# One batch alone ahead of the first scores: the other batches' first norms go into the unit loop of a decoder kernel

## The chip, the core and the metric

The kernel runs on one core of a Trainium2 chip. The metric is the device time of one launch in microseconds (us). A core has five engines that run their own instruction streams and wait for each other at semaphores: TensorE (PE: matrix products and transposes into PSUM), VectorE (DVE), ScalarE (ACT: activations, also plain copies), GpSimd (POOL) and SyncE (SP), which here only issues DMA transfers.

## The reference, cut to what matters

Six sublayers follow each other, each with a residual and a layer norm without weights in front. x is 4 batches of 512 rows of 128 numbers. Only the start of the first sublayer matters here:

```python
x = x + _L0_attn_ref(_layernorm(x, axis=-1), W_in, b_in, W_out, b_out)

P = X @ W_in + b_in                        # 16 heads, each with Q, K, V, G of 64
d2 = q2[..., :, None] + k2[..., None, :] - 2.0 * qk
W = jnp.power(EPS + jnp.sqrt(jnp.maximum(d2, 0.0)), -2)
W = W / (EPS + jnp.sum(W, axis=-1, keepdims=True))
A = jnp.einsum('hbts,hbse->hbte', W, V)
H = G * A                                  # then heads side by side, @ W_out + b_out
```

q2 and k2 are the squared norms of the rows of Q and K. After it come a cross attention, a mixture of experts with its own attention, a windowed attention, a second cross attention and a quantized feed-forward layer; the change doesn't touch them.

## The kernel before, in words

The first sublayer runs in 32 units: a unit is one batch and one pair of heads, batch by batch, so units 0 to 7 read batch 0 alone, units 8 to 15 batch 1, and so on. The normalized and transposed rows of all batches lie in `XT` (128 numbers on the partitions, 512 rows per batch).

For a unit TensorE makes K, Q, V and G by projections from `XT[:, b]` (`project_pair`, `project_values_and_gates`), the squared norms q2 and k2 (`query_norms`, `key_norms`), the scores in eight PSUM banks (`scores`: first a product with the split q2 in bf16, then Q against K), the weighted values and the row sums of the weights of the unit before, and from unit 2 on a piece of the output projection. VectorE evacuates K and Q and forms their squares (`evacuate_pair`, four operations), evacuates V and G, and adds k2 to the scores and clips them (`guard`, eight operations of 128x512, called guards below). ScalarE takes root, logarithm and exponential of the 128x4096 distances of a unit in six passes, changes its function table twice in each unit, and takes the reciprocal of the row sums in the same way. GpSimd splits q2 into three bf16 pieces (`split_norms`, four operations), adds up the weights of a unit for the row sums (`sum_weights`, three operations) and scales the gates.

The projections of unit u + 2 stand behind the scores of unit u in the loop; those of unit 1 stand in unit 0, also behind the scores. The squares of Q go through one buffer, and so does the copy of q2 (`QX`).

The order on each engine is written out by hand: each engine has a function that issues its instructions in program order, and nothing is reordered. `psum_jobs` lists all uses of PSUM banks in TensorE's order; `place_jobs` gives them banks in turn and works out which semaphores a use must wait for until its bank has been read.

Ahead of the loop every engine works on all four batches of the first layer norm (numbered `(0, b)`): VectorE forms statistics (`stats`) and normalizes (`normalize`), ScalarE makes the reciprocal deviation from the variance (`rstd`, one logarithm, one exponential), TensorE transposes (`ln_turn`), ScalarE copies to `XT` (`xt_out`). GpSimd adds the output bias to the rows of `X` once they have been normalized (line 2741). SyncE issues the transfers on one queue in program order: batch 0, the constants, batches 1 to 3, the biases, the weights of head pair 0, then the value bias `BV` and the weights of the seven other pairs.

`after_batch(u, n)` names the batch whose last unit lies n + 1 units back; by it later norms already stand inside the loop.

## Time and profile before

| what | us |
|---|---|
| median of 3 runs (1272.89 to 1273.5) | 1272.97 |
| the profiled execution | 1272.73 |
| its span in the trace | 1270.8 |
| busy: TensorE, VectorE, ScalarE, GpSimd | 1128.9, 901.9, 879.7, 627.9 |
| first transposes, first projection, first scores (start) | 9.45, 16.11, 27.59 |
| scores of units 1, 2 (start) | 48.60, 63.91 |

The profiled execution has 1.9 us outside its span. The page cuts the span into 40 slices of 32 us; the busy share of a slice stands as a digit in tenths. In the first slice TensorE has a 4, in the second an 8, and from there a 9 until the unit loop ends near 560 us:

```profile
PE   4899999999999999987888898799997999985765
DVE  5766667766767677657888978546746786878885
ACT  2799999999989998992666767755564676733311
POOL 2577777777767777595455545013330300054232
```

### The profile page before, as it was taken

How to read it: one execution, taken by the hardware profiler on the slowest of the kernel's cores; microseconds unless marked ns; L12 is line 12 of the kernel's file. 1: busy time of each engine (PE TensorE's matmuls, PEld its weight loads, DVE VectorE, ACT ScalarE, POOL GpSimd, SP SyncE). 2: the span in 40 equal slices, each digit the busy share in tenths (PEclk: the TensorE clock that was granted, in tenths of full speed). 3: DMA queues.
4: the chain of work that ended last, by engine and by line, in shares of the span. 5: the costliest groups of instructions: out<-in, count | busy, mean ns of one | idle time of the engine just before them, and what ended most of it. 6: DMA issues, size and time to landing. Idle time of an engine off the chain costs nothing.

```text
span 1270.8 us, 17038 instructions
## 1 busy us (share of the span) xinstructions
PE 1128.9 (89%) x6055; PEld 589.1 (46%) x6055; DVE 901.9 (71%) x1756; ACT 879.7 (69%) x1150; POOL 627.9 (49%) x463
## 2 busy tenths in 40 slices
PE   4899999999999999987888898799997999985765
PEld 2444444444444444432333332277775676653444
DVE  5766667766767677657888978546746786878885
ACT  2799999999989998992666767755564676733311
POOL 2577777777767777595455545013330300054232
PEclk9999999999999999996889989999998999997877
DMA  7200000000000000020000000000001000000000
GB/s 178 66 1 2 1 1 1 1 1 1 1 1 1 1 1 1 1 68 1 18 1 1 1 1 1 2 1 1 1 1 63 1 1 1 1 1 0 1 9 25
DMA packets 25631, 14.47 MB, mean 11 GB/s; under 512 B 14558, under 2 KB 24396, under 8 KB 25420
## 3 DMA queue, kind: packets, MB, share of 16 engines
q1 hardware_dynamic: 25548, 13.39, 3.7%
q8 instruction: 49, 0.80, 0.2%
q14 instruction: 34, 0.28, 0.1%
HBM read 12.34 MB, written 1.05 MB: 11 GB/s over the span
## 4 chain that ended last, share of the span: by engine, by line
PE 31%; POOL 31%; issue 20%; DVE 16%; ACT 1%; DMA 0%; POOLq 0%; SPq 0%; ACTq 0%; DVEq 0%
DVE ARENA L1159 6%; POOL ARENA L2711 6%; POOL ARENA L2709 6%; POOL ARENA L2705 6%; PE PS L1030 5%; POOL WQ L2722 3%; POOL ARENA L2735 3%; PE PS L900 3%; PE PS L1414 2%; PE PS L1004 2%; PE PS L832 2%; PE PS L1438 2%; PE PS L848 2%; PE PS L1405 2%; POOL WQ L2724 2%
## 5 line engine op out<-in xcount | busy, mean ns | idle before, releaser
L2565 DVE TENSOR_SCALAR ARENA<-PS,ARENA 128x512 f32<-128x512 f32 x256 | 174.5, 744 | 66.7 <-PE PS L2199 66.3
L1159 DVE TENSOR_REDUCE ARENA<-PS 128x1 f32<-128x512 f32 x256 | 160.9, 683 | 28.2 <-PE PS L848 27.7
L1075 ACT ACTIVATE ARENA<-PS 128x1024 f32<-128x1024 f32 x128 | 128.9, 1026 | 61.9 <-PE PS L886 61.6
L2378 ACT ACTIVATE ARENA<-ARENA 128x2048 f32<-128x2048 f32 x64 | 122.2, 1912 | 60.6 <-DVE ARENA L2565 60.1
L2199 PE MATMUL PS<-ARENA 64*128 64x512 f32 x512 | 129.0, 623 | 0.0
L2385 ACT ACTIVATE ARENA<-ARENA,consts_sb 128x2048 f32<-128x2048 f32 x64 | 124.6, 1994 | 0.4
L2209 PE MATMUL PS<-ARENA 128*64 128x512 f32 x512 | 118.7, 606 | 1.3 <-issue 1.3
L2391 ACT ACTIVATE ARENA<-ARENA 128x2048 f32<-128x2048 f32 x64 | 118.4, 1898 | 0.0
L2718 POOL TENSOR_SCALAR WQ<-ARENA,consts_sb 128x512 bf16<-128x512 f32 x32 | 22.3, 696 | 159.1 <-DVE ARENA L2541 159.1
L1340 POOL TENSOR_TENSOR ARENA<-ARENA 128x512 f32<-128x512 f32 x32 | 40.7, 1271 | 121.4 <-DVE ARENA L1298 120.9
L848 PE MATMUL PS<-ARENA 32*128 32x512 bf16 x256 | 74.0, 415 | 24.9 <-DVE ARENA L1159 19.8
L2541 DVE TENSOR_SCALAR ARENA<-PS 128x512 f32<-128x512 f32 x32 | 22.1, 692 | 95.3 <-PE PS L2175 95.3
L900 PE MATMUL PS<-ARENA 128*32 128x512 f32 x512 | 73.2, 645 | 8.9 <-issue 7.9
L2711 POOL TENSOR_TENSOR ARENA<-ARENA 128x1024 f32<-128x1024 f32 x32 | 76.0, 2375 | 2.5
L2709 POOL TENSOR_TENSOR ARENA<-ARENA 128x1024 f32<-128x1024 f32 x32 | 75.8, 2370 | 0.0
L2705 POOL TENSOR_TENSOR ARENA<-ARENA 128x1024 f32<-128x1024 f32 x32 | 75.7, 2365 | 0.0
L2209 PEld LDWEIGHTS PS<-ARENA 128*64 128x64 f32 x512 | 34.7, 138 | 81.1 <-issue 81.1
L1312 POOL TENSOR_SCALAR ARENA<-ARENA,consts_sb 128x512 bf16<-128x512 f32 x32 | 21.8, 695 | 100.3 <-ACT ARENA L1057 100.3
L1030 PEld LDWEIGHTS PS<-W,ARENA 128*128 128x128 f32 x512 | 59.5, 191 | 21.2 <-issue 19.0
L1106 ACT ACTIVATE ARENA<-PS,ARENA 128x512 f32<-128x512 f32 x64 | 40.4, 684 | 37.4 <-PE PS L1004 37.4
L1030 PE MATMUL PS<-W,ARENA 128*128 128x128 f32 x512 | 65.3, 281 | 0.8 <-ACT ARENA L1106 0.7
L848 PEld LDWEIGHTS PS<-ARENA 32*128 32x128 bf16 x256 | 17.5, 92 | 104.3 <-DVE ARENA L1159 64.0
(301 smaller groups left out, 2606.3 us busy)
## 6 DMA issues: line engine op xcount, KB each, us to landing
ARENA<-in_window_bias_dram SPq DMA_DIRECT2D x1, 1536.0 KB, 6.3
WKVG<-in_L_attn_W_in_dram SPq DMA_DIRECT2D x3, 448.0 KB, 5.6
X<-in_x_dram SPq DMA_DIRECT2D x4, 256.0 KB, 5.4
W<-in_L_ffn_w_dram SPq DMA_DIRECT2D x1, 1024.0 KB
out_dram<-X SPq DMA_DIRECT2D x4, 256.0 KB, 2.3
BV<-in_L_attn_b_in_dram SPq DMA_DIRECT2D x1, 512.0 KB, 6.7
Wout<-in_L_attn_W_out_dram SPq DMA_DIRECT2D x1, 512.0 KB, 4.7
WQ<-in_L_attn_wq_dram SPq DMA_DIRECT2D x1, 512.0 KB, 3.3
```

Source lines behind the costliest of these rows:

```text
L1030: mm = pe.matmul(o[:, t * P:(t + 1) * P], H1[:, i % 2, c, t * P:(t + 1) * P], W2[:, e, c, :], start=c == 0, stop=c == 1)
L1075: act.activation(PT[m % PT_SLOTS], bank(("cP", m)), ACT.Exp, scale=0.5).then_inc(sem("c_exp"), 1)
L1159: dve.tensor_reduce(NMX[:, w % 2, t, h:h + 1], bank(("cS", n, j)), AX.X, ALU.max, negate=True).then_inc(sem("c_max"), 1)
L2199: done(pe.matmul(banks[c], SK[r, u % 2, kt * P:(kt + 1) * P], MQ[r, u % 2, :], start=False, stop=True), ("S", u, c))
L2209: mm = pe.matmul(o[hd * 64:hd * 64 + 64, :], VA[:, u % 3, kt, hd * 64:hd * 64 + 64], D[:, u % 2, kt, hd, :], start=kt == 0, stop=kt == QT - 1)
L2378: act.activation(chunk(u, half), chunk(u, half), ACT.Sqrt).then_inc(sem("rooted"), 1)
L2385: act.activation(chunk(u, half), chunk(u, half), ACT.Ln, bias=const("eps_w")).then_inc(sem("logged"), 1)
L2391: act.activation(chunk(u, half), chunk(u, half), ACT.Exp, scale=-2.0).then_inc(sem("w_ready"), 1)
L2565: dve.tensor_scalar(D[:, u % 2, kt, hd, :], bank(("S", u, c)), K2[:, u % 2, kt, hd:hd + 1], 1e-30, ALU.add, ALU.max).then_inc(sem("guarded ...
L2705: pool.tensor_tensor(WSUM[:, u % 2], D[:, u % 2, 0], D[:, u % 2, 1], ALU.add).then_inc(sem("w_paired"), 1)
L2709: pool.tensor_tensor(WPAIR, D[:, u % 2, 2], D[:, u % 2, 3], ALU.add).then_inc(sem("w_paired"), 1)
L2711: pool.tensor_tensor(WSUM[:, u % 2], WSUM[:, u % 2], WPAIR, ALU.add).then_inc(sem("w_summed"), 1)
```

## The change

Only batch 0 goes through its first norm ahead of the loop. A new function `first_norm(u, units_after)` gives the batch whose first norm has a step in unit u: statistics in units 0, 1, 2 (batches 1, 2, 3), the deviation in units 1, 2, 3, normalization in units 2, 3, 4, transposes and copy in units 3, 4, 5; GpSimd's bias addition too in units 3, 4, 5. The projections of unit 1 and VectorE's evacuation of them stand ahead of the scores of unit 0 instead of behind them; its norms q2 and k2 stay behind. GpSimd splits the norms of unit 1 ahead of the bias addition and the clearing of three buffers (the `memset` lines), and those of unit 2 behind them. SyncE takes the weights of head pair 1 as a transfer group of its own (`win_next_in`), and issues batches 1 to 3 behind it, ahead of the weights of pairs 2 to 7. ScalarE loads its function table ahead of the wait for the constants. Batch 3 is normalized into the room of batch 0 in `Y`, since its own room holds the squares of Q.

```diff
+def first_norm(u, units_after):
+
+    b = u - units_after + 1
+    return b if 1 <= b < B else None
...
-            for heads, name in ((slice(0, 2), "win_first_in"), (slice(2, H0), "win_in")):
-                if name == "win_in":
+            for heads, name in ((slice(0, 2), "win_first_in"), (slice(2, 4), "win_next_in"), (slice(4, H0), "win_in")):
+                if name == "win_next_in":
...
+                if name == "win_next_in":
+                    for b in range(1, B):
+                        stream_in(b)
...
             def project_pair(u):
                 b, p = divmod(u, PAIRS)
+                if p == 0:
+                    pe.wait_ge(sem("xt_ready"), norm_no(0, b))
...
             pe.wait_ge(sem("consts_in"), 16)
-            for b in range(B):
-                ln_turn(0, b)
+            ln_turn(0, 0)
...
             key_norms(0)
+            pe.wait_ge(sem("win_next_in"), 16 * 4)
+            project_pair(1)
             pe.wait_ge(sem("pieces_set"), 1)
             for u in range(UNITS):
                 scores(u, 0)
                 scores(u, 1)
                 if u == 0:
-                    pe.wait_ge(sem("win_in"), 16 * 4)
-                    project_pair(1)
                     query_norms(1)
                     key_norms(1)
+                    pe.wait_ge(sem("win_in"), 16 * 4)
...
+                if first_norm(u, 3) is not None:
+                    ln_turn(0, first_norm(u, 3))
...
+                if first_norm(u, 1) is not None:
+                    rstd(0, first_norm(u, 1))
+                if first_norm(u, 3) is not None:
+                    xt_out(0, first_norm(u, 3))
...
+            act.preload_act_table_set("natural_log_exp_and_others")
             act.wait_ge(sem("consts_in"), 16)
-            act.preload_act_table_set("natural_log_exp_and_others")
-            for b in range(B):
-                rstd(0, b)
-            for b in range(B):
-                xt_out(0, b)
+            rstd(0, 0)
+            xt_out(0, 0)
...
-            layernorm(0)
+            stats(0, 0)
+            normalize(0, 0)
...
-            full(dve, ("ln", 0, B - 1))
...
             key_norms(0)
+            evacuate_pair(1)
...
                 if u == 0:
-                    evacuate_pair(1)
...
+                if first_norm(u, 0) is not None:
+                    stats(0, first_norm(u, 0))
+                if first_norm(u, 2) is not None:
+                    normalize(0, first_norm(u, 2))
...
             split_norms(0)
+            split_norms(1)
...
             pool.wait_ge(sem("bcast_in"), 32)
-            for b in range(B):
-                pool.wait_ge(sem("ln_y"), b + 1)
...
-            pool.wait_ge(sem("x_biased"), B)
+            add_bias(0)
             for t in (WX, VC0, TMX):
                 pool.memset(t, 0.0).then_inc(sem("c_init"), 1)
-            for u in range(1, 3):
-                split_norms(u)
+            split_norms(2)
             for u in range(UNITS):
                 sum_weights(u)
+                if first_norm(u, 3) is not None:
+                    add_bias(first_norm(u, 3))
```

GpSimd, from the end of the split of unit 0 to the start of that of unit 2, or as far as twelve rows reach; L2741 and L2760 are the bias additions, L2745 and L2766 the clearing. Before:

```order
L2728 TENSOR_TENSOR ARENA<-WQ 128x512
L2741 TENSOR_TENSOR X<-X,Bout 128x512 x4
L2745 MEMSET ARENA 128x1024
L2745 MEMSET ARENA 128x2048
L2745 MEMSET ARENA 128x1024
L2718 TENSOR_SCALAR WQ<-ARENA,consts_sb 128x512
L2722 TENSOR_TENSOR WQ<-ARENA,WQ 128x512
L2724 TENSOR_SCALAR WQ<-WQ,consts_sb 128x512
L2728 TENSOR_TENSOR ARENA<-WQ 128x512
L2718 TENSOR_SCALAR WQ<-ARENA,consts_sb 128x512
```

And on the same engine in the changed kernel:

```order
L2746 TENSOR_TENSOR ARENA<-WQ 128x512
L2736 TENSOR_SCALAR WQ<-ARENA,consts_sb 128x512
L2740 TENSOR_TENSOR WQ<-ARENA,WQ 128x512
L2742 TENSOR_SCALAR WQ<-WQ,consts_sb 128x512
L2746 TENSOR_TENSOR ARENA<-WQ 128x512
L2760 TENSOR_TENSOR X<-X,Bout 128x512
L2766 MEMSET ARENA 128x1024
L2766 MEMSET ARENA 128x2048
L2766 MEMSET ARENA 128x1024
L2736 TENSOR_SCALAR WQ<-ARENA,consts_sb 128x512
```

The split of unit 1 has moved ahead of the bias and the clearing, and three of the four bias additions are gone from here.

TensorE, from the key norms of unit 0 on (the x4 on consts_sb,ARENA); the rows on PIECES and on ARENA are the scores, XT with WKVG or WQ the projections of K and Q. Before:

```order
L2181 MATMUL PS<-consts_sb,ARENA 128x128 x4
L2195 MATMUL PS<-ARENA,PIECES 128x512 x4
L2199 MATMUL PS<-ARENA 128x512 x4
L2195 MATMUL PS<-ARENA,PIECES 128x512 x4
L2199 MATMUL PS<-ARENA 128x512 x4
L2156 MATMUL PS<-XT,WKVG 128x512
L2159 MATMUL PS<-XT,WQ 128x512
L2175 MATMUL PS<-Y,consts_sb 128x512
L2181 MATMUL PS<-consts_sb,ARENA 128x128 x4
```

On the same engine after the change:

```order
L2198 MATMUL PS<-consts_sb,ARENA 128x128 x4
L2173 MATMUL PS<-XT,WKVG 128x512
L2176 MATMUL PS<-XT,WQ 128x512
L2212 MATMUL PS<-ARENA,PIECES 128x512 x4
L2216 MATMUL PS<-ARENA 128x512 x4
L2212 MATMUL PS<-ARENA,PIECES 128x512 x4
L2216 MATMUL PS<-ARENA 128x512 x4
L2192 MATMUL PS<-Y,consts_sb 128x512
L2198 MATMUL PS<-consts_sb,ARENA 128x128 x4
```

The two projections of unit 1 have moved ahead of the scores of unit 0, and the norms of unit 1 follow the scores directly.

VectorE at the end of unit 2 in the changed kernel, from the copy of q2 of unit 4 to the guards of unit 3 (before, the copy of k2 and the guards are neighbours there):

```order
L2555 TENSOR_SCALAR ARENA<-PS 128x512
L2567 COPY ARENA<-PS 128x8
L2514 BN_STATS STAT<-X 128x6 x4
L2517 BN_AGGR MV<-STAT 128x2 x4
L2524 TENSOR_SCALAR Y<-X,MV,RSTD 128x128 x4
L2579 TENSOR_SCALAR ARENA<-PS,ARENA 128x512 x8
```

The statistics of batch 3 and the normalization of batch 1 stand between the norms and the guards.

## Rows read from the trace of the kernel before

**Rows 1.** The page's groups: line, engine, operation, count, busy us, mean ns.

```profile
L2385 ACT ACTIVATE ARENA<-ARENA,consts_sb 128x2048 f32<-128x2048 f32 x64 | 124.6, 1994 | 0.4
...
L2541 DVE TENSOR_SCALAR ARENA<-PS 128x512 f32<-128x512 f32 x32 | 22.1, 692 | 95.3 <-PE PS L2175 95.3
```

**Rows 2.** Timeline of VectorE, start: start us, us, line, operation, count, [idle before].

```profile
3.73 0.87 DVE L2493 BATCH_NORM_STATS2 STAT<-X 128x6 f32<-128x128 f32 x4 [3.73 <-DMA X<-in_x_dram]
4.64 0.38 DVE L2496 BATCH_NORM_AGGREGATE MV<-STAT 128x2 f32<-128x6 f32 x4
...
8.22 1.09 DVE L2503 TENSOR_SCALAR Y<-X,MV,RSTD 128x128 f32<-128x128 f32 x4
```

**Rows 3.** Timeline of ScalarE, start.

```profile
4.99 1.28 ACT L2441 ACT_TABLE_LOAD   x1 [4.99 <-DMA consts_sb<-in_consts_dram]
6.29 0.30 ACT L2364 ACTIVATE RSTD<-MV,consts_sb 128x4 f32<-128x4 f32 x1
...
15.92 0.59 ACT L2371 COPY XT<-PS 128x512 f32<-128x512 f32 x1 [0.44 <-PE PS L2143]
```

**Rows 4.** Timeline of TensorE, start.

```profile
9.45 1.08 PE L2143 MATMUL PS<-consts_sb,Y 128*128 128x128 f32 x4 [9.45 <-DVE Y L2503]
...
16.11 2.07 PE L2156 MATMUL PS<-XT,WKVG 128*128 128x512 f32 x2
...
27.59 0.74 PE L2195 MATMUL PS<-ARENA,PIECES 32*128 32x512 bf16 x4 [4.00 <-issue]
```

**Rows 5.** DMA issues until 45 us: count, KB each, median us to landing.

```profile
BV<-in_L_attn_b_in_dram SPq DMA_DIRECT2D x1, 512.0 KB, 6.7
...
WKVG<-in_L_attn_W_in_dram SPq DMA_DIRECT2D x3, 64.0 KB, 2.5
```

**Rows 6.** Timeline of SyncE's issues, start.

```profile
5.86 1.49 SPq L2069 DMA_DIRECT2D WKVG<-in_L_attn_W_in_dram  x3
...
9.61 7.26 SPq L2069 DMA_DIRECT2D WKVG<-in_L_attn_W_in_dram  x3
```

**Rows 7.** Timeline of GpSimd, 23 to 60 us.

```profile
23.53 0.69 POOL L2718 TENSOR_SCALAR WQ<-ARENA,consts_sb 128x512 bf16<-128x512 f32 x1 [21.67 <-DVE ARENA L2541]
...
27.45 4.93 POOL L2741 TENSOR_TENSOR X<-X,Bout 128x512 f32<-128x512 f32 x4
32.45 3.59 POOL L2745 MEMSET ARENA<- 128x1024 f32 x3
...
52.53 2.36 POOL L2705 TENSOR_TENSOR ARENA<-ARENA 128x1024 f32<-128x1024 f32 x1
```

**Rows 8.** Timeline of TensorE, units 1 and 2.

```profile
48.60 0.39 PE L2195 MATMUL PS<-ARENA,PIECES 32*128 32x512 bf16 x4
...
57.52 3.65 PE L2209 MATMUL PS<-ARENA 128*64 128x512 f32 x16
61.01 1.03 PE L2217 MATMUL PS<-ARENA,consts_sb 128*64 128x512 f32 x4
...
63.91 0.40 PE L2195 MATMUL PS<-ARENA,PIECES 32*128 32x512 bf16 x4
```

**Rows 9.** Timeline of VectorE, behind the guards of unit 1.

```profile
55.74 0.74 DVE L2518 TENSOR_SCALAR ARENA<-PS,BKP 128x512 f32<-128x512 f32 x1
```

**Rows 10.** Windows: length, busy us per engine, clock; last two: units 11, 12.

```profile
36.50:39.10 2.60, 0.01 (x1) 0.01 (x1) 2.54 (x4) 2.58 (x2) 0.00 (x0) 1.00 0.98 267
39.10:42.60 3.50, 3.50 (x11) 2.47 (x12) 0.69 (x1) 3.49 (x3) 0.70 (x1) 0.53 0.01 1
211.65:227.89 16.24, 15.97 (x78) 7.29 (x78) 11.42 (x19) 15.51 (x11) 11.98 (x9) 1.00 0.00 1
227.89:244.52 16.63, 16.36 (x82) 7.68 (x83) 12.29 (x20) 15.48 (x12) 12.19 (x9) 1.00 0.00 0
```

**Rows 11.** Timeline of VectorE around the guards of units 12 and 13.

```profile
227.19 2.20 DVE L2503 TENSOR_SCALAR Y<-X,MV,RSTD 128x128 f32<-128x128 f32 x4
...
246.10 0.75 DVE L2565 TENSOR_SCALAR ARENA<-PS,ARENA 128x512 f32<-128x512 f32 x1 [2.21 <-PE PS L2199]
```

More of the change, by code:

```diff
@@ L662, in decoder_kernel, with normal_rows @@
         QSQ = Y[:, B - 1].rearrange("p t d -> p (t d)")
+        def normal_rows(k, b):
+            return Y[:, 0 if (k, b) == (0, B - 1) else b]
         assert at <= 31412
@@ L2147, in ln_turn @@
                 pe.wait_ge(sem("ln_y"), norm_no(k, b))
-                transposes(("ln", k, b), Y[:, b])
+                transposes(("ln", k, b), normal_rows(k, b))
             def wpair(p, kind):
@@ L2737, in _, with add_bias @@
             split_norms(0)
-            pool.wait_ge(sem("bcast_in"), 32)
-            for b in range(B):
-                pool.wait_ge(sem("ln_y"), b + 1)
+            split_norms(1)
+            def add_bias(b):
+                pool.wait_ge(sem("ln_y"), norm_no(0, b))
                 pool.tensor_tensor(X[:, b], X[:, b], Bout[:].unsqueeze(1).to_broadcast([P, QT, P]),
                                    ALU.add).then_inc(sem("x_biased"), 1)
-            pool.wait_ge(sem("x_biased"), B)
+            pool.wait_ge(sem("bcast_in"), 32)
+            add_bias(0)
             for t in (WX, VC0, TMX):
                 pool.memset(t, 0.0).then_inc(sem("c_init"), 1)
-            for u in range(1, 3):
-                split_norms(u)
+            split_norms(2)
             for u in range(UNITS):
                 sum_weights(u)
+                if first_norm(u, 3) is not None:
+                    add_bias(first_norm(u, 3))
                 if u + 3 < UNITS:
```

21 lines of the change are left out of this document (8 added, 13 removed).

## The prediction

> **What bounds the kernel now.** I read the page's slices first, then the timelines of each engine over the first 80 us (where the change moves most), then windows that cut the unit loop at the starts of the scores. In the loop over the 32 units TensorE is the bound: between the scores of units 11 and 12 it works 15.97 of 16.24 us [rows 10]. So anything that reaches TensorE earlier is kept to the end, and anything added to TensorE in the loop is paid.
>
> The start isn't bound by TensorE. VectorE gets batch 0 at 3.73 us and has its statistics at 5.02 [rows 2]; ScalarE loads its table only after the constants have landed, and takes the logarithm at 6.29 [rows 3]; batch 0 is normalized at 8.22, because VectorE was on batch 1 in between [rows 2]. TensorE then turns four batches, and the first projection starts at 16.11, though it reads batch 0 alone [rows 4]. From there to the first scores (27.59) it is a chain: project, evacuate, norms, and the split on GpSimd, which starts at 23.53 [rows 4, 7]. After the scores of unit 0 the next long wait is again GpSimd: it adds the bias to four batches (4.93), clears (3.59), and splits unit 1 and unit 2 before it comes to the weights of unit 0 at 52.53. TensorE takes the row sums of unit 0 at 61.01, when GpSimd has them, and the scores of unit 2 start at 63.91 [rows 7, 8]. From there TensorE is the bound. So I work out when the scores of unit 2 start in the changed kernel, and then what units 2 to 5 cost more.
>
> **Part 1, to the first scores.** Statistics of batch 0 end at 5.02, as before. The table is now loaded ahead of the wait for the constants, so the logarithm can start when both are there, near 5.1: the table load was seen to wait until 4.99 for the constants [rows 3]. Logarithm 0.30, an exponential on the same four numbers, hand-offs: 5.7. Normalize 1.09: 6.8. Four transposes 1.08: 8.0. Copy 0.59: 8.6, and with the hand-off the first projection can start at 8.75 instead of 16.11 [rows 2 to 4].
>
> Does something else come last there? On the sync queue the three other batches are gone from ahead of the weights (three issues of half a microsecond each), so the 64 KB slices of the first pair, issued until 7.35 before, are issued until 5.8, and with the 2.5 us to landing they are there at 8.3 [rows 5, 6]. That is just ahead of 8.75. BV is needed near 14.5; issued at 5.8 to 6.3 with its 6.7 [rows 5] it lands at 13. The weights of the second pair follow behind it and are needed at 16.5 to 17.5.
>
> From the first projection to the scores it was 27.59 - 16.11 = 11.48. The chain is the same, but TensorE is at its low pace for longer, since it now comes from idle: 2.07 us for the K projection is already the low pace [rows 4] (the clock column shows no record so early; the duration tells it), and before, the pace came up in the middle of the Q projection. Now V and G can be slow too, some 0.9 each, of which VectorE's evacuation of Q covers about 0.6. So 11.75 if the pace comes up early, 12.75 if late; I take 12.25, the middle. First scores at 8.75 + 12.25 = 21.0 (20.5 to 21.5).
>
> The second unit's projections and their evacuation (four VectorE operations of up to 0.74 [rows 9]) go under GpSimd's split of 3.92 us [rows 7], where TensorE and VectorE were idle: nothing.
>
> **Part 2, from the scores of unit 0 (call it s) to those of unit 2.** The guards end 7.14 after a warm start (48.60 to 55.74) [rows 8, 9], the norms' copy takes 0.69 [rows 1], so GpSimd starts the split of unit 1 at s + 7.9. From there it never waits: split 3.96, one bias 1.24 (4.93 / 4), clears 3.6, split 4.0, three sums of 2.36 (7.15 with gaps) [rows 7]. The sum is 20.0: row sums at s + 27.9. The split of unit 2 finds its input (TensorE has made it by s + 12), and the first sum its weights: behind the guards ScalarE has one more root, a table of 1.28, two logarithms and two exponentials, none over 1.99 [rows 1, 3], so all are done by s + 18.4, and the sums begin at s + 20.8. TensorE has the scores of unit 1 at about s + 12.8 (12.41 from scores to row sums in unit 1, less 3.5 of weighted values, plus two pairs of norms, 1.9 each) and is at the row sums 12.41 later, at s + 25.3 [rows 8]: it waits 2.6 us. From the row sums to the next scores 63.91 - 61.01 = 2.9 [rows 8]. Scores of unit 2 at s + 30.9 = 51.9, against 63.91: 12.0 earlier. What was late before (four biases ahead of the split, the projections of unit 1 behind the scores) is gone; what is late next is GpSimd's own work.
>
> **Part 3, what the loop pays.** (a) Three groups of transposes more on TensorE, in units 3, 4, 5. Unit 12 has just that: 16.63 against 16.24, so 0.39 each, 1.2 in all [rows 10]. (b) On VectorE the statistics (0.87 + 0.38 [rows 2]) come behind the norms of units 0, 1, 2, and the normalization behind those of 2, 3, 4. The room there is the 2.21 us that VectorE waits for the scores [rows 11] (about 1.3 in units 0 and 1, where no output piece stands behind the norms). Statistics alone fit. A normalization in this place took 2.20 us, not the 1.09 of the start [rows 2, 11]: GpSimd splits at that time. It just fits alone (units 3 and 4; in unit 4 a small copy comes on top, 0.2), but in unit 2 both come: 1.2 + 2.2 - 2.2 = 1.2 late, between 0.1 (if it took 1.09) and 1.2; I take 1.2, the nearer row. TensorE's second half of the scores needs the banks that the guards free, so I let it pass in full. (c) ScalarE gets at most 1.1 more in a unit (a pair of small activations, a copy of 0.59), and is busy for 15.51 of 16.24, with 0.39 more to come; the bias additions (1.24) go into GpSimd's wait, 11.98 of 16.24 busy [rows 10]: nothing. Sum: 1.2 + 1.2 + 0.2 = 2.6.
>
> Here the Trainium skill bears: SBUF — State Buffer, section "SBUF: two separate sides", says that VectorE and GpSimd share one pair of ports as an exclusive lock, and that the loser is blocked for the whole instruction. The two durations of the same operation above agree with it. By that rule alone, each of the four pieces could wait for a whole GpSimd operation of 1.2 us, and unit 2 would lose up to some 4 us instead of 1.2; the measured 2.20 decides here.
>
> **Part 4, the pace.** TensorE now has two idle gaps: 2.0 us before the first scores (it has done unit 1's projections by about 19) and 2.6 before the row sums of unit 0. After the gap of 2.60 at 36.50 the granted clock fell, and 3.50 us went at about half of it (0.53) [rows 10], which costs some 1.7. I take that for the gap of 2.6, not for that of 2.0. Both ends: 0 and 3.4. The Trainium skill (TensorE: Matmul & The Clock Gate, section "Why this matters for your kernels") warns only of idle gaps longer than both of these; by it the cost would be 0 (rival A), while the row shows a fall after 2.60.
>
> **Sum.** -12.0 + 2.6 + 1.7 = -7.7. The profiled execution took 1272.73 us (0.24 under the median); 1265.0, against the median 1265.2. The rest of the program has the same instructions in the same order, shifted.
>
> **The rivals.**
> A, the pace holds in both gaps: 1.7 less, 1263.6. For it: both gaps are short, and in their stretch TensorE is busier than before. Chance 0.2.
> B, it falls in both, or in one of them while the weights land a little late: another 1.7, 1266.9. For it: the fall after 2.60. Chance 0.2.
> C, the loop swallows more: each of three batches costs what the crowded unit 2 costs and the transposes, as where VectorE holds up the scores: 3 x (1.2 + 0.39) + 2 from a normalization that waits longer beside the sums, about 6.8 instead of 2.6, so 1269.4. For it: the doubled 2.20. Against it: unit 12 costs only 0.39 with the same normalization in front of it. 0.1.
> D, slower: the weights of the pairs 2 to 7 stand behind all of the second pair's and the three batches on the sync queue, and TensorE has the projection of unit 2 right behind the norms of unit 1, at s + 7.2 = 28.2; the whole TensorE queue stands behind that wait. The issue of the 448 KB slices stalls, 7.26 us for three until 16.9 [rows 6], and with the 6.7 us of BV to landing the last is there near 23.5; the same bytes are ahead of it now. It decides only if they land after 28.2, and the gain is gone when they land 7.7 later than that, at 36; at 40 the kernel is at 1277. 0.03.
> The forecast has 0.4. The other 0.07 lies between C and no change, mostly a late landing of some part of the first weights.
>
> **How the numbers follow.** About 0.2% (2.5 us) is what a measurement of this kernel can tell from no change. The forecast, A, B and C all are faster by more: 0.90, and a part of the rest: 0.92. Within: 0.05. Slower: 0.03. The range reaches below A by the half microsecond of the first scores and a cheap unit 2: 1262.2; above to B and half way into C: 1268.8.
>
> **What would show it.** The first projection near 8.8; the first scores near 21 with VectorE's second unit done before them; GpSimd without a gap from the split of unit 1 to the sums of unit 0; TensorE waiting 2 to 3 us for them, the scores of unit 2 near 52; a wait for VectorE at the scores of unit 3 and a period 0.4 longer in units 3 to 5; from unit 6 on each start about 7.7 us earlier. Wrong would be: the first projection waiting for weights after 9.5, a wait at unit 2's projection for a DMA, or a shift that keeps shrinking after unit 5.

## The result, and the profile after

| what | before | changed kernel |
|---|---|---|
| median of 5 runs each, us | 1272.89 (1271.22 to 1273.5) | 1265.47 (1265.02 to 1266.25) |
| ratio, 95% interval | | 0.9946 (0.9933 to 0.996) |
| the profiled execution / its span, us | 1272.73 / 1270.8 | 1266.25 / 1264.4 |

The changed kernel is 7.4 us faster; 7.7 were forecast. Where the time came from is read from the starts of the scores, unit by unit, which cut the loop in both traces at the same instruction:

| start of the scores of unit | before, us | after, us | difference |
|---|---|---|---|
| 0 | 27.59 | 20.81 | -6.78 |
| 1 | 48.60 | 33.92 | -14.68 |
| 2 | 63.91 | 52.92 | -10.99 |
| 3 | 80.16 | 69.37 | -10.79 |
| 4 | 96.39 | 86.60 | -9.79 |
| 5 | 113.31 | 104.10 | -9.21 |
| 6 to 20 | 129.54 ... 361.50 | 122.37 ... 354.34 | -7.17 |
| 21 | 380.26 | 373.95 | -6.31 |
| 29 | 517.49 | 511.90 | -5.59 |
| end of the span | 1270.8 | 1264.4 | -6.4 |

11 us are won by unit 2, 3.8 are given back by unit 6. By unit 29 another 1.6 net are gone: units 20 and 28 take 0.86 and 0.99, and unit 26 gives 0.27 back. The change touches none of the three. (Unit 26 took 16.92 in the three traced kernels with all four norms ahead of the loop and 16.65 in the nine others; why wasn't followed up.)

The start, on VectorE and ScalarE in the changed kernel's timelines (start, us, engine, line, operation, count, and in brackets the idle time before and who ended it), which answers to [rows 2, 3]:

```profile
3.82 0.87 DVE L2514 BATCH_NORM_STATS2 STAT<-X 128x6 f32<-128x128 f32 x4 [3.82 <-DMA X<-in_x_dram]
4.72 0.38 DVE L2517 BATCH_NORM_AGGREGATE MV<-STAT 128x2 f32<-128x6 f32 x4
5.77 1.12 DVE L2524 TENSOR_SCALAR Y<-X,MV,RSTD 128x128 f32<-128x128 f32 x4 [0.67 <-ACT RSTD L2385]
```

```profile
0.73 1.28 ACT L2463 ACT_TABLE_LOAD   x1 [0.73 <-PEq L2791]
5.20 0.30 ACT L2383 ACTIVATE RSTD<-MV,consts_sb 128x4 f32<-128x4 f32 x1 [3.19 <-DVE MV L2517]
```

The normalization of batch 0 starts at 5.77 instead of 8.22. TensorE's timeline, which answers to [rows 4] and, from 42.84 on, to [rows 8]:

```profile
7.04 1.08 PE L2158 MATMUL PS<-consts_sb,Y 128*128 128x128 f32 x4 [7.04 <-DVE Y L2524]
...
8.89 2.05 PE L2173 MATMUL PS<-XT,WKVG 128*128 128x512 f32 x2 [0.47 <-ACT XT L2390]
...
20.81 0.40 PE L2212 MATMUL PS<-ARENA,PIECES 32*128 32x512 bf16 x4 [2.28 <-issue]
...
42.84 3.65 PE L2226 MATMUL PS<-ARENA 128*64 128x512 f32 x16
48.59 1.08 PE L2234 MATMUL PS<-ARENA,consts_sb 128*64 128x512 f32 x4 [2.10 <-POOL ARENA L2729]
49.60 1.68 PE L2192 MATMUL PS<-Y,consts_sb 128*128 128x512 f32 x2
51.07 1.91 PE L2198 MATMUL PS<-consts_sb,ARENA 128*128 128x128 f32 x8
```

The first projection waits for ScalarE's copy, not for weights. The row sums of unit 0 wait 2.10 us for GpSimd, and behind that wait the norms take 1.68 and 1.91 us, which take 1.12 and 1.05 in the second profile below: the granted clock of the stretch is 0.67 (first window below), so TensorE spent most of it at the lower of its two clock levels (1.2 and 2.4 GHz). GpSimd's timeline, which answers to [rows 7]:

```profile
28.73 0.69 POOL L2736 TENSOR_SCALAR WQ<-ARENA,consts_sb 128x512 bf16<-128x512 f32 x1 [8.02 <-DVE ARENA L2555]
...
32.67 1.28 POOL L2760 TENSOR_TENSOR X<-X,Bout 128x512 f32<-128x512 f32 x1
33.89 3.59 POOL L2766 MEMSET ARENA<- 128x1024 f32 x3
...
46.18 2.35 POOL L2729 TENSOR_TENSOR ARENA<-ARENA 128x1024 f32<-128x1024 f32 x1
```

From 28.73 to 48.5 it has no gap, but 8.02 us of idle time stand just ahead. The windows (length, then busy time of each engine, granted clock, DMA share, GB/s) are the row sums and norms behind TensorE's wait; unit 2; unit 12, which answers to the last of [rows 10]; and unit 20:

```profile
48.59:52.92 4.33, 4.33 (x16) 2.45 (x17) 0.69 (x1) 3.58 (x6) 0.73 (x2) 0.67 0.01 0
52.92:69.37 16.45, 16.18 (x77) 7.29 (x77) 12.74 (x30) 14.22 (x13) 12.04 (x9) 0.98 0.01 2
220.72:237.35 16.63, 16.36 (x82) 7.68 (x82) 12.31 (x20) 15.49 (x12) 12.11 (x9) 1.00 0.00 0
354.34:373.95 19.61, 17.84 (x81) 7.90 (x80) 14.24 (x29) 14.37 (x14) 12.05 (x9) 0.91 0.00 0
```

Unit 12 is what it was. What the loop gives back shows on VectorE, at the end of unit 2 and of unit 4; the normalizations there answer to [rows 11]:

```profile
69.86 1.79 DVE L2524 TENSOR_SCALAR Y<-X,MV,RSTD 128x128 f32<-128x128 f32 x4
71.57 2.71 DVE L2579 TENSOR_SCALAR ARENA<-PS,ARENA 128x512 f32<-128x512 f32 x4
...
103.40 2.19 DVE L2524 TENSOR_SCALAR Y<-X,MV,RSTD 128x128 f32<-128x128 f32 x4
105.51 0.18 DVE L2670 COPY BN<-PS 128x38 f32<-128x38 f32 x1
```

And on TensorE right behind (the scores of unit 5):

```profile
105.75 0.39 PE L2212 MATMUL PS<-ARENA,PIECES 32*128 32x512 bf16 x3 [1.27 <-DVE BN L2670]
```

The scores of unit 5 take their second bank from the transposed bias columns. VectorE's small copy (BN, 0.18 us) empties it, and that copy stands behind the normalization of 2.19 us.

### The profile page after: what moved, and what is told of

The parts are those of the page before. It is cut to its first block, busy times and chain, and to the rows that moved or that the text cites. A ratio compares the mean times of both kernels' runs of the same rounds, so it can differ in the third digit from the quotient of the medians.

```text
span 1264.4 us, 17047 instructions
## 1 busy us (share of the span) xinstructions
PE 1128.7 (89%) x6055; PEld 588.6 (47%) x6055; DVE 904.6 (72%) x1756; ACT 879.9 (70%) x1150; POOL 628.3 (50%) x463
## 3 DMA queue, kind: packets, MB, share of 16 engines
HBM read 12.34 MB, written 1.05 MB: 11 GB/s over the span
## 4 chain that ended last, share of the span: by engine, by line
PE 32%; POOL 31%; issue 20%; DVE 15%; ACT 1%; POOLq 0%; DMA 0%; ACTq 0%; DVEq 0%
DVE ARENA L1170 6%; POOL ARENA L2729 6%; POOL ARENA L2727 6%; POOL ARENA L2723 6%; PE PS L1041 5%; POOL WQ L2740 3%; POOL ARENA L2753 3%; PE PS L911 3%; PE PS L1425 2%; PE PS L1015 2%; PE PS L843 2%; PE PS L1449 2%; PE PS L1416 2%; PE PS L859 2%; POOL WQ L2742 2%
## 5 line engine op out<-in xcount | busy, mean ns | idle before, releaser
L2216 PEld LDWEIGHTS PS<-ARENA 64*128 64x128 f32 x512 | 44.9, 189 | 46.0 <-issue 46.0
L859 PEld LDWEIGHTS PS<-ARENA 32*128 32x128 bf16 x256 | 17.6, 92 | 104.2 <-DVE ARENA L1170 64.0
```

Of the source, the lines that this page charges most:

```text
L2216: done(pe.matmul(banks[c], SK[r, u % 2, kt * P:(kt + 1) * P], MQ[r, u % 2, :], start=False, stop=True), ("S", u, c))
```

## The experiments

All were timed in 5 rounds beside the kernel before, which gave 4 to 12 executions of each; ratios are to the kernel before, with 95% intervals. The changed kernel stands at 0.9946 (0.9933 to 0.996) in its own series and at 0.9929 (0.9915 to 0.9942) in the last one. The intervals of the variants with the clears moved, the copy ahead, the normalization ahead, both edits, and the other batches loaded first overlap one or both of the changed kernel's. Their totals don't settle a difference from it, so what they show is read from the units of one traced execution each. "Unit n" is the time from the scores of unit n to those of unit n+1.

**GpSimd's clears in its idle time.**

```diff
             split_norms(0)
-            split_norms(1)
...
             add_bias(0)
             for t in (WX, VC0, TMX):
                 pool.memset(t, 0.0).then_inc(sem("c_init"), 1)
+            split_norms(1)
             split_norms(2)
```

> The changed kernel, but GpSimd adds the bias to batch 0 and clears its three tiles (1.28 + 3.59 us) straight behind the split of unit 0, and then splits units 1 and 2. Theory: from 28.73 to the row sums at 48.59 GpSimd works without a gap and sets their start, while it idles 8.02 us before that; with 4.9 us of work moved into the idle stretch the row sums come up to the 2.1 us earlier that TensorE waits, the clock doesn't fall behind them (1.4 us in the row sums and norms of that stretch), and the split of unit 1 may start up to 0.3 later. Scores of unit 2 near 49.6 instead of 52.9; about 3.3 us less than the changed kernel, near 1262. Rival (the whole gain is the 7.2 us by which the first projection starts earlier, and what lies between first scores and unit 6 is noise of the same size): no change, 1265.5.

Measured: 1262.01 (1255.72 to 1268.16, the widest spread of all), ratio 0.9917 (0.9892 to 0.9941). The scores of unit 2 start at 49.56, 3.36 earlier, as expected: GpSimd's work between the guards and the row sums was what the changed kernel waited for. The end didn't follow: unit 3 took 19.80 instead of 17.23, and from unit 4 on the profiled execution is only 0.6 earlier. VectorE, GpSimd and TensorE there:

```profile
66.69 2.71 DVE L2524 TENSOR_SCALAR Y<-X,MV,RSTD 128x128 f32<-128x128 f32 x4
```

```profile
66.09 1.16 POOL L2740 TENSOR_TENSOR WQ<-ARENA,WQ 128x512 f32<-128x512 f32 x1
...
68.16 1.16 POOL L2746 TENSOR_TENSOR ARENA<-WQ 128x512 bf16<-128x512 f32 x1
```

```profile
70.12 0.39 PE L2212 MATMUL PS<-ARENA,PIECES 32*128 32x512 bf16 x1 [1.28 <-DVE ARENA L2579]
...
71.09 3.45 PE L2216 MATMUL PS<-ARENA 64*128 64x512 f32 x8
```

The normalization of unit 2 took 2.71 beside GpSimd's split (1.79 in the changed kernel), the guards came later by that, TensorE waited 1.28, and its scores went at 3.45 instead of 1.99. So the gain at unit 2 was right, and the total right by its median, but in the execution that the trace shows the loop swallowed 2.8 of the 3.4 us, 2.6 of them in unit 3. Against the second profile of the changed kernel (last experiment), in which the clock didn't fall, this execution is 1.9 earlier at unit 2 and 1.1 later at unit 4.

The edit doesn't explain the 2.71. In the changed kernel's second profile the normalization stands in the same place of the same split, 0.60 us behind the start of its second operation:

```profile
68.23 1.71 DVE L2524 TENSOR_SCALAR Y<-X,MV,RSTD 128x128 f32<-128x128 f32 x4
```

```profile
67.62 1.16 POOL L2740 TENSOR_TENSOR WQ<-ARENA,WQ 128x512 f32<-128x512 f32 x1
...
69.69 1.26 POOL L2746 TENSOR_TENSOR ARENA<-WQ 128x512 bf16<-128x512 f32 x1
```

The first three of its four instructions took the same in both traces, to 0.01 us. The fourth took 0.33 there and 1.33 here, beside the same operation of GpSimd (L2746). The section on the hardware counts how often that happens.

**The copy of the bias columns ahead of the normalization.**

```diff
                     evacuate_gates(u + 1)
+                if u == 4:
+                    full(dve, ("tb", 1))
+                    dve.tensor_copy(BN[:, 0:N_COLS], bank(("tb", 1))[:, 0:N_COLS]).then_inc(sem("bias_cols"), 1)
                 if u + 2 < UNITS:
                     query_norms(u + 2)
                     key_norms(u + 2)
```

> The changed kernel, but in unit 4 VectorE's copy of the bias columns (0.18 us, it frees a bank that the scores of unit 5 wait for) stands ahead of the norms and of the normalization of batch 3, not behind them. Theory: the wait of 1.27 us of TensorE inside the scores of unit 5 is all due to the normalization of 2.19 us in front of that copy, so unit 5 takes about 16.6 instead of 18.27 and every later start is some 1.5 earlier: 1264.0. Rival (VectorE is simply full in that unit, and the normalization holds up the guards and the scores in any order): the wait turns up at another instruction, within 0.3 us of the changed kernel, 1265.3.

Measured: 1262.87 (1261.73 to 1265.4), ratio 0.9931 (0.992 to 0.9943). Unit 5 took 16.62 instead of 18.27, and TensorE has no wait there; every unit from 6 to 10 has the length it had. (Unit 4 took 17.77 instead of 17.50, with a normalization of 2.65 instead of 2.20 in it; see the section on the hardware.) The theory holds: 1.65 us by one copy of 0.18 us in the wrong place. The ratio alone wouldn't tell, since the spread is as large; the unit's length does.

**The projections of unit 1 behind the first scores again.**

```diff
             key_norms(0)
-            pe.wait_ge(sem("win_next_in"), 16 * 4)
-            project_pair(1)
...
                 if u == 0:
+                    pe.wait_ge(sem("win_next_in"), 16 * 4)
+                    project_pair(1)
                     query_norms(1)
                     key_norms(1)
```

VectorE's evacuation of them moves back with them.

> The changed kernel, but the projections of unit 1 and their evacuation stand again behind the scores of unit 0. Theory: GpSimd's chain to the row sums starts with the split of unit 1, which waits for the norms of unit 1; the projections (two of 0.5 to 1) and their evacuation (four operations of VectorE, up to 0.74) put 4 to 5 us between the guards and that split, so the row sums and the scores of unit 2 come 4 to 5 later: about 1270. TensorE idles more, so the clock may cost another 1 to 1.5. Rival (the first projection's earlier start alone makes the gain, and the order of unit 1 is covered by other waits): no change, 1265.5.

Measured: 1270.1 (1263.28 to 1275.47), ratio 0.998 (0.9966 to 0.9994). Scores of unit 0 at 21.07, of unit 1 at 42.12, of unit 2 at 58.01, 5.1 later than in the changed kernel, and 4.8 later from unit 3 to 20. TensorE's timeline says how:

```profile
21.07 0.74 PE L2212 MATMUL PS<-ARENA,PIECES 32*128 32x512 bf16 x4 [3.99 <-issue]
...
32.62 1.78 PE L2192 MATMUL PS<-Y,consts_sb 128*128 128x512 f32 x2 [2.68 <-DVE Y L2541]
34.19 1.91 PE L2198 MATMUL PS<-consts_sb,ARENA 128*128 128x128 f32 x8
...
55.05 1.08 PE L2234 MATMUL PS<-ARENA,consts_sb 128*64 128x512 f32 x4 [0.35 <-POOL ARENA L2729]
```

The row sums wait only 0.35 for GpSimd here. TensorE was late by itself: a wait of 2.68 for VectorE, and behind it the norms at 1.78 and 1.91. From the first scores to those of unit 2 this kernel takes 36.94 us and the one before 36.32, though GpSimd has one bias addition here and four there. The trace of the kernel before has the same two low stretches on TensorE, behind 4.00 us ahead of the first scores and behind 2.67:

```profile
28.26 3.78 PE L2199 MATMUL PS<-ARENA 64*128 64x512 f32 x8
...
39.09 1.93 PE L2175 MATMUL PS<-Y,consts_sb 128*128 128x512 f32 x2 [2.67 <-DVE Y L2527]
40.81 1.92 PE L2181 MATMUL PS<-consts_sb,ARENA 128*128 128x128 f32 x8
```

And on GpSimd, behind the additions and clears (which end at 36.04), and at the last sum of unit 0:

```profile
41.85 0.70 POOL L2718 TENSOR_SCALAR WQ<-ARENA,consts_sb 128x512 bf16<-128x512 f32 x1 [5.81 <-DVE ARENA L2541]
...
57.30 2.38 POOL L2711 TENSOR_TENSOR ARENA<-ARENA 128x1024 f32<-128x1024 f32 x1
```

So in the kernel before, GpSimd's four additions and three clears cost nothing: behind them it still waited 5.81 us for the norms of unit 1.

**All four first norms ahead of the loop, the rest as changed.**

```diff
-    jobs += ln_job(0, 0, "A")
+    for b in range(B):
+        jobs += ln_job(0, b, "A")
...
-            ln_turn(0, 0)
+            for b in range(B):
+                ln_turn(0, b)
...
-            add_bias(0)
+            for b in range(B):
+                add_bias(b)
```

The same on ScalarE and VectorE, no first norm in any unit, and the batches loaded first.

> The changed kernel, but all four batches are normalized and turned ahead of the loop again, with the bias added to all four ahead of GpSimd's clears, as before the change; the projections of unit 1 stay ahead of the first scores and GpSimd splits unit 1 ahead of the biases. Theory: first scores near 27.5, GpSimd's chain with four biases (4.93 instead of 1.28) gives the row sums 31.4 behind them, scores of unit 2 near 62; no transposes and no normalization in units 2 to 5, so their 3.6 us are not paid. In all 1270.5 to 1271.5, about 5.5 more than the changed kernel and 2 less than before. Rival (moving unit 1's projections alone is worth what GpSimd's late start cost, about 4): 1268.5. Rival (the gain is all in the first projection): as before, 1273.

Measured: 1273.62 (1265.11 to 1275.01), ratio 1.0003 (0.999 to 1.0015). Missed by 2 to 3 us. The number is that of the last rival, but not by its reason: the run before this one has the early first projection and keeps only 2.4 us of the gain. The first scores came at 26.83, the row sums 32.26 behind them (expected 31.4), and then:

```profile
59.09 1.97 PE L2234 MATMUL PS<-ARENA,consts_sb 128*64 128x512 f32 x4 [5.75 <-POOL ARENA L2736]
60.99 2.08 PE L2192 MATMUL PS<-Y,consts_sb 128*128 128x512 f32 x2
62.86 1.92 PE L2198 MATMUL PS<-consts_sb,ARENA 128*128 128x128 f32 x8
```

TensorE waits 5.75 us, and the row sums and norms then take 5.61 instead of the 2.9 of [rows 8]; those 2.7 I hadn't counted. The 0.9 by which the row sums came later than expected is the clock as well: unit 0 took 13.93 instead of 13.10, and GpSimd's split of unit 1 started 8.75 behind the first scores instead of 7.92. Scores of unit 2 at 64.70, against 63.91 before. So the projections of unit 1 ahead of the scores bring nothing here while GpSimd has four biases to add in between: they turn TensorE's own delay into a wait for GpSimd, and the clock falls behind that. Without the two falls (3.5 us together) the scores of unit 2 would stand near 61.2; one of the twelve executions took 1265.11, 8.5 under the median, and no trace shows it. By medians the early start with the old order of unit 1 is worth 2.4 us, the new order with the old start nothing, and both together 7.4.

**Statistics and normalization ahead of the norms.**

```diff
-                if u + 2 < UNITS:
-                    query_norms(u + 2)
-                    key_norms(u + 2)
                 if first_norm(u, 0) is not None:
                     stats(0, first_norm(u, 0))
                 if first_norm(u, 2) is not None:
                     normalize(0, first_norm(u, 2))
+                if u + 2 < UNITS:
+                    query_norms(u + 2)
+                    key_norms(u + 2)
```

> The changed kernel, but in units 0 to 4 the statistics and the normalization of another batch stand on VectorE ahead of the norms of unit u+2, in the 2.8 to 3.9 us in which it waits for TensorE's squares, not behind them. Theory: what the loop pays on VectorE comes from the place: behind the norms GpSimd splits at the same time, and the guards and the copy of the bias columns stand behind. Ahead of the norms a normalization takes about 1.1 and not 1.8 to 2.2, nothing is late in unit 2, and the copy of the bias columns finds its bank in time: the 0.6 of the crowded unit and the 1.65 of unit 5 go, the transposes (0.39 each) stay; 2.2 less, 1263.3. Rival (VectorE's total work in those units is the cost, wherever it stands; then the norms come late and with them the split and the next unit): within 0.5 of the changed kernel, 1265.5.

Measured: 1261.98 (1260.46 to 1262.7), ratio 0.9917 (0.9904 to 0.993). Unit 3 took 16.63 (17.23 in the changed kernel), unit 5 16.63 (18.27): 2.24 us together, as expected, and both are now just the 16.24 with the 0.39 of the transposes. VectorE in unit 3:

```profile
79.60 1.10 DVE L2524 TENSOR_SCALAR Y<-X,MV,RSTD 128x128 f32<-128x128 f32 x4
82.89 0.69 DVE L2555 TENSOR_SCALAR ARENA<-PS 128x512 f32<-128x512 f32 x1 [2.19 <-PE PS L2192]
```

The normalization takes 1.10, in time that VectorE idled through. In unit 4 the moved normalization took 1.85, beside a bias addition of GpSimd, and that cost nothing. The rest of its lead in the traces (unit 1 17.61 instead of 19.00, and 0.8 and 1.0 in units 20 and 28) is the clock, below.

**Both: the clears in GpSimd's idle time and the normalizations ahead.** The edits are the two above.

> The kernel before this one with GpSimd's one bias and three clears behind the split of unit 0 besides. The run with the clears alone put the scores of unit 2 3.4 us earlier, but lost 2.6 of it in unit 3, where a normalization of 2.71 beside GpSimd's split held the guards up, TensorE waited 1.28 and its clock fell. Theory: with the normalization ahead of the norms that wait can't arise, and both gains add: scores of unit 2 near 49.5, of unit 6 near 116.8 (122.4 less 3.4 and 2.2), 5.6 less than the changed kernel: about 1259.8. Rival (the earlier start is given back in unit 3 in any case, to a wait that the profile hides behind VectorE's): unit 6 near 119.5, 1262.5.

Measured: 1260.65 (1260.17 to 1261.43), ratio 0.9909 (0.9896 to 0.9921), near the theory's 1259.8 and away from the rival's 1262.5. Unit 1 took 15.31, unit 3 16.63, and no scores wait for VectorE beyond the 0.27 of any unit. Scores of unit 6 at 117.82 (116.8 by the theory, 119.5 by the rival). Scores of unit 2 at 50.41 and not at 49.5: unit 0 took 14.26 instead of 13.11, since in this execution the clock fell behind the wait before the first scores.

**The other batches loaded ahead of the weights.**

```diff
             stream_in(0)
             sp.dma_start(C[:], a["consts"]).then_inc(sem("consts_in"), 16)
+            for b in range(1, B):
+                stream_in(b)
...
-                if name == "win_next_in":
-                    for b in range(1, B):
-                        stream_in(b)
```

> The changed kernel, but the three other batches of x are loaded ahead of the weights on the sync queue again. Theory (as forecast): the weights of the first pair are then issued until about 7.3 and land 2.5 later, so the first projection waits for them until 9.8 or 9.9 instead of starting at 8.89, and all that follows to the first scores, and with them GpSimd's chain, comes about 1.0 later: 1266.4. Rival (landing times are not set by the place in the queue): 8.9 and no change, 1265.5. Rival (the bias that is broadcast lands late as well, and holds the values): 1.5 to 2.5 more.

Measured: 1265.66 (1263.97 to 1270.32), ratio 0.995 (0.9936 to 0.9964). The first projection does wait for the weights:

```profile
9.36 2.07 PE L2172 MATMUL PS<-XT,WKVG 128*128 128x512 f32 x2 [0.30 <-DMA WKVG<-in_L_attn_W_in_dram]
```

It starts 0.47 later than in the changed kernel, and the first scores 0.51 later (21.32). But 0.38 of that was there before: the logarithm waited for the constants until 5.58, 0.38 later than in the changed kernel, and it did so until 5.77 and 5.53 in two variants whose loads are in the changed kernel's order. From the transposes to the first projection it is 1.94 here and 1.85 in the changed kernel, so in this execution the weights themselves cost 0.09; had the constants landed as early as there, and the weights when they did here, it would be 0.47. Either is under the 1.0 expected, and no more than the spread of the runs, so the median can't confirm it.

**The table ahead of the constants, alone.**

```diff
+            act.preload_act_table_set("natural_log_exp_and_others")
             act.wait_ge(sem("consts_in"), 16)
-            act.preload_act_table_set("natural_log_exp_and_others")
```

> The kernel before, with ScalarE's table loaded ahead of the wait for the constants, and nothing else. Theory: the logarithm starts near 5.2 instead of 6.29, but the first normalization stands behind the statistics of batch 1 on VectorE (8.22), so nothing behind it moves: within 0.3 us of before. Rival (the table's place is part of the gain): up to 1.1 less.

Measured: 1271.68 (1270.57 to 1273.73), ratio 0.9998 (0.9989 to 1.0007). The logarithm starts at 5.13, and the first normalization still stands behind batch 1's statistics on VectorE, which wait for the landing of batch 1:

```profile
6.35 0.87 DVE L2493 BATCH_NORM_STATS2 STAT<-X 128x6 f32<-128x128 f32 x4 [1.32 <-DMA X<-in_x_dram]
...
7.56 1.08 DVE L2503 TENSOR_SCALAR Y<-X,MV,RSTD 128x128 f32<-128x128 f32 x4
```

Batch 1 landed 0.66 earlier in this execution than in the profiled one of before. I take that for the spread between executions (in the kernel with all four norms ahead it landed 0.43 earlier); no run here shows its cause. With a first projection in which the clock rose sooner (1.72 and 1.02 for K and Q, 2.07 and 1.44 in the profile of before) it puts the first scores at 26.20 instead of 27.59: so much does the start of the kernel before vary, a fifth of the 6.8 us that the changed kernel's first scores are ahead. By the median, the table's place is no part of the gain by itself.

**The later normalizations ahead of the norms as well.** To the kernel with both edits:

```diff
                 if first_norm(u, 2) is not None:
                     normalize(0, first_norm(u, 2))
+                if after_batch(u, 2) is not None:
+                    normalize(1, after_batch(u, 2))
+                if after_batch(u, 12) is not None:
+                    normalize(2, after_batch(u, 12))
                 if u + 2 < UNITS:
                     query_norms(u + 2)
                     key_norms(u + 2)
```

> The kernel with the first normalizations ahead of the norms and the clears in GpSimd's wait, and the later normalizations (of the second and third norm, units 11, 19, 27 and 21, 29) ahead of the norms on VectorE as well. Theory: in units 19 and 27 a normalization of 2.21 beside GpSimd's split stands with an addition and statistics (0.68 + 0.87 + 0.38) ahead of the guards of the next scores, and TensorE waits 1.75 and 1.77 us for those in units 20 and 28; the clock falls behind that wait in some executions (0.85 to 1.0 more). With the normalization in the 3.9 us in which VectorE waits for the squares, both waits go: unit 20 about 17.0 instead of 18.77, unit 28 about 17.8 instead of 19.55, and no fall of the clock in either; 3.5 us less than without, up to 5.4 against executions in which it fell: about 1256.5. Rival (the additions and statistics alone fill that place, so that TensorE waits as long for them): 1260.5.

Measured: 1252.04 (1250.81 to 1259.79), ratio 0.9849 (0.9826 to 0.9872): 20.7 us under the kernel before, the fastest of all. Unit 20 took 16.65 and unit 28 17.43; both waits are gone. It did better than expected by 4.5. By the starts of the scores 7.0 us are won up to unit 31 against the kernel without this edit, of which 3.3 in unit 20 (its clock had fallen there), 2.1 in unit 28 and 1.4 ahead of unit 2 (mostly clock again); 1.9 more of the span lie behind the loop and weren't followed up. Against executions in which the clock didn't fall, units 20 and 28 are 2.1 shorter each: 4.2 us is what the place of the normalizations shows for itself.

**The changed kernel once more.** No edit.

> The changed kernel once more, unedited, beside its variants and on their chip. Every theory: 1265.5. What it tells apart is where its executions differ: the theory that a wait of 1.75 to 2.3 us of TensorE makes the clock fall in some executions and not in others expects units 1, 20 and 28 at either of two lengths (17.6 or 19.0, 18.77 or 19.6, 19.55 or 20.5), and every other unit within 0.02 of the first profile; the rival (the spread comes from transfers) expects other units to differ.

Measured: 1263.55 (1262.99 to 1264.39). The profiled execution is 3.2 us shorter in its span (1261.2). Four units make 3.4 of it: unit 1 took 17.61 instead of 19.00, unit 2 16.24 instead of 16.45, unit 20 18.78 instead of 19.61, unit 28 19.55 instead of 20.52. Units 3 and 30 are 0.08 shorter each, every other unit agrees within 0.02, and the stages behind the loop are 0.4 longer. The row sums waited as long:

```profile
48.54 1.08 PE L2234 MATMUL PS<-ARENA,consts_sb 128*64 128x512 f32 x4 [2.08 <-POOL ARENA L2729]
49.55 1.12 PE L2192 MATMUL PS<-Y,consts_sb 128*128 128x512 f32 x2
50.51 1.05 PE L2198 MATMUL PS<-consts_sb,ARENA 128*128 128x128 f32 x8
```

The same wait, and no slow norms behind it. Its windows of units 2 and 20, with the clock at 1.00 where the first profile had 0.98 and 0.91:

```profile
51.50:67.74 16.24, 15.97 (x78) 7.23 (x78) 12.74 (x30) 15.59 (x13) 12.76 (x10) 1.00 0.01 2
352.64:371.42 18.78, 16.75 (x83) 7.78 (x83) 14.14 (x29) 14.37 (x14) 12.05 (x9) 1.00 0.00 0
```

## Why the prediction was right, step by step

| step | forecast | first profile | the same without the clock's falls |
|---|---|---|---|
| first projection | 8.75 | 8.89 | 8.9 |
| first scores | 21.0 | 20.81 | 20.79 |
| row sums behind the first scores | 27.9 | 27.78 | 27.75 |
| scores of unit 2 against before | -12.0 | (-11.0) | -12.4 |
| loop, units 2 to 5 | +2.6 | +3.6 | +3.6 |
| clock at the row sums | +1.7 | +1.6 | 0 |

The last column is the second profile of the changed kernel. In the first, -12.4 + 3.6 + 1.6 gives the -7.2 that stand from unit 6 to 20; units 20, 26, 28 and 30 take 1.7 back (20 and 28 by the clock, 1.8 together), the stages behind the loop give 0.9, which was not followed up: -6.4 in the span. So a part of the agreement is errors that cancel: the loop was priced 1.0 too low, and what lies behind it wasn't priced.

**Part 1 held.** The first projection's time came out of the durations of [rows 2 to 4] within 0.15 us. From there to the first scores it took 11.92, not 12.25: V and G weren't slow (1.09 and 1.02), and this and the 0.14 on the other side are why 21.0 came so close. The weights were there in time; with three batches ahead of them on the queue TensorE waits 0.30 for them, which is worth 0.1 to 0.5 and not the 1.0 expected. The table's place alone changes nothing where VectorE's order decides, as that expectation said; in the changed kernel the logarithm waits for the statistics and no longer for the table (5.20, 3.19 idle), which no run isolates.

**Part 2 came out right by its sum, with a wrong reading beside it.** The forecast of GpSimd's chain from the guards to the row sums was off by 0.1 us, and moving 4.9 us out of that chain brought unit 2 forward by 3.4, of which 1.4 are the clock's fall that went with the wait. But the prediction says that in the kernel before TensorE takes the row sums "when GpSimd has them", and calls that the next long wait. It wasn't one: GpSimd's last sum ends at 59.68 (57.30 + 2.38), and TensorE comes from 3.65 us of weighted values at 61.01 with no idle time [rows 8]. What was late in the kernel before was TensorE's own chain through unit 1: the scores of unit 0 at the low pace (3.78 instead of 1.99 for their first half, behind the 4.00 us ahead of them), the wait for VectorE, the low pace behind that too, and so scores of unit 1 only 21.01 behind those of unit 0. The kernel with the projections of unit 1 behind the first scores shows it, with the same waits and the same paces. So "what was late before (four biases ahead of the split, ...)" is wrong for the biases: they were hidden then, and would have become the bound only through the other half of the change. The sum didn't rest on that sentence, since it was built forward from the guards; the expectation for all four norms ahead did rest on it in part, and missed.

**Part 3 was too low by 1.0, in two terms that partly cancel.** The copy of the bias columns was priced at 0.2, its own duration, and cost 1.65: what counted was not its length but what stands ahead of it and who waits for the bank that it frees. The crowded unit 2 was priced at 1.2 and cost 0.61, since the normalization took 1.79 there, not 2.20. Unit 4 cost 0.58, of which 0.39 for the transposes; the other 0.19 stays in every variant with the transposes in the loop, also where no normalization stands behind the norms, and its cause is open. The transposes' 0.39 each is what units 3 and 5 keep when the rest is taken away. The mechanism behind the 1.2, a normalization made longer by GpSimd's split, was right: in the clears' profiled execution it took 2.71, and unit 3 paid 2.6 (0.9 of waiting, the rest at a granted clock of 0.69 behind the wait); the run with the normalization elsewhere paid nothing.

**Part 4 was right in size, and in one profile of two.** The fall behind the wait for the row sums cost 1.39 + 0.21 = 1.6 (forecast 1.7), and none came behind the 2.28 us before the first scores. But in the second series the traced execution was rival A's case: no fall in either, forecast 1263.6, measured 1263.03 (median 1263.55). That this is so close is luck in part, since rival A prices the loop 1.0 too low as well. Forecast and rival A are one kernel; which of them an execution shows is decided anew. The Trainium skill (TensorE: Matmul & The Clock Gate, section "Why this matters for your kernels") warns only of idle gaps longer than these. The rows of the first profile, 4.33 us at a granted clock of 0.67 behind a wait of 2.10, show a fall all the same, and the measurement decides.

**Rivals B, C and D.** Not C: the loop cost 3.6, not 6.8. Not D: nothing at unit 2's projection waits for weights. B (another 1.7 from the clock) is nearest to what units 20 and 28 added, 0.85 and 0.97 in the first profile, in a place that no rival named. A slip in the range: half way from B into C is 1268.2, not 1268.8; nothing rests on it.

## What to carry to other kernels

A small instruction that frees a buffer is priced by what stands ahead of it on its engine, not by its own length. Work added to a full loop belongs where its engine waits for the bound engine, and not behind the hand-off that sets the others running: the same normalization cost TensorE 0.6 to 1.65 us in one place and nothing in the other, and moving the old ones there too won another 4.2 us in the two units concerned (8.6 by the medians of two series, with the clock and a part behind the loop that wasn't followed up). Before a wait is blamed for the time before a change, look whether the engine that is the bound stood idle there at all.

## What the runs showed of the hardware

**The clock after a short wait is not the same in every execution.** In the twelve profiles of this study a unit comes out short or long wherever TensorE has a wait of about 2 us. Behind the 2.28 us before the first scores: 13.1 in six executions, 13.93 to 14.26 in three. Behind the 2.1 before the row sums: 17.6 in four, 19.00 in one. Behind 1.75 to 1.77 in unit 20: 18.77 in seven, 19.56 to 19.94 in four. Behind the longer waits it fell in every execution that has them: behind 2.67 in unit 0 and behind 4.00 before the first scores in three of three (the kernel before, the one with the table moved, and the one with unit 1's projections behind the scores), behind 5.75 in the one execution that has it, the norms behind it at a granted clock of 0.50. Behind 1.27 to 1.28 it held in unit 5 of five executions and fell once in unit 3. For the short ones, work and wait are the same to 0.04 us, so the wait alone doesn't decide; what does stays open. The part of the gain that comes from the shorter waits in unit 0 is therefore partly clock: the change replaces two waits behind which the clock always fell by one of 2.28 and one of 2.10 behind which it mostly held. Each fall behind a wait of about 2 us cost 0.8 to 1.6 us, up to a fifth of the effect measured here; between the two profiles of the changed kernel it is all but 0.2 of the difference in the loop. Some executions differ by more, down to 1255.72 and up to 1268.16 in one kernel, and no trace shows those.

**VectorE and GpSimd slow each other unevenly, and not the same way each time.** The same four normalizing instructions took 1.08 to 1.12 us with GpSimd idle. Where they start 0.60 us behind the split's second operation (unit 2) they took 1.71 to 1.79 in five executions and 2.71 in one; where they start 0.19 behind its first (the other units) they took 2.19 to 2.21 in 61 cases and 2.65 in six, in three different executions. Within each group the starts agree to 0.01 us, so the place in the split sets which pair of lengths it is, and not which of the two; what does stays open. In each long case one instruction of 0.33 took 1.33, beside an operation of GpSimd that then took its usual 1.16; in the short ones that operation took 1.26. No step of the split grew by more than 0.12. The Trainium skill (SBUF — State Buffer, section "SBUF: two separate sides") describes the ports that the two share as a lock that one of them holds for a whole instruction; an instruction that comes 1.0 late beside an operation of 1.16 agrees with it.

What it costs depends on who waits: 0.26 us in unit 12 (16.89 instead of 16.63), 0.44 in unit 28 in one execution (19.99 instead of 19.55, behind a wait of 2.21, with no fall of the clock), and 2.6 in unit 3 of the kernel with the clears moved, most of it by the clock.
